# Passes moved from behind a run of four doubles to the head of it, in a DLRM tower on one core

## The chip, the cores and the metric

The kernel runs on one core of a Trainium2 chip. The metric is the device time of one execution in microseconds (us), of which the median of several runs is taken. TensorE (PE) does the matrix products, VectorE (DVE) and ScalarE (ACT) work on its results, GpSimd (POOL) issues the gathers from the embedding tables, and SyncE (SP) issues the other transfers.

## What is computed

A batch of 1024 rows looks up 32 fields of 64 numbers each. For every one of the 496 pairs of fields a 64x64 matrix of the weights stands between the two, which gives one number per pair and row; these and 16 dense numbers go through a tower of three layers.

```python
e = jnp.stack([tbl_0[ids[:, 0]], ..., tbl_31[ids[:, 31]]], axis=1)   # 1024 x 32 x 64
p = e[:, ROW]                                  # the 496 pairs of fields, ROW < COL
q = e[:, COL]
kp = jnp.einsum('bpj,ipj->bpi', p, kernel)     # 64x64 for each pair
z = jnp.sum(kp * q, axis=-1)                   # 1024 x 496
h = jnp.concatenate([z, dense_ctx], axis=1)    # 1024 x 512
h = jnp.maximum(h @ W_top1 + b_top1, 0.0)
h = jnp.maximum(h @ W_top2 + b_top2, 0.0)
y = h @ W_top3
```

## The kernel before

The batch is cut into 4 blocks of 256 rows. Two fields make a tile, so a block has 16 tiles; the 64 tiles of all blocks are gathered by POOL (line 419, four gathers a tile), turned by PE (a transpose, line 644, into `t_ps`) and copied to `rows` by ACT (line 492). In block 0 three tiles are looked up by a product with one-hot rows instead (line 666). From the second block on two tiles are turned at a time.

The pairs are worked off in **pieces**, 62 a block and 248 in all. Each piece is four products on PE into one of the three buffers of `u_ps` (URING), which DVE multiplies with the other field. There are two kinds:

- A **double** (48 a block; line 690, or line 697 for the two of a block that take the fields of a tile with each other, here called self doubles). DVE writes its product to `prod` (lines 607, 610), a ring of 8. Two doubles make a **quad**: PE adds them up along the partitions with a small selector (`add_up`, lines 724 and 730) into `z_ps`.
- A **pass** (14 a block; line 711), where the batch rows stand on the partitions. DVE writes its product to `pass_prod` (line 618), a ring of 3, and ACT adds it up along the row, 16 sums a pass (line 504, `add_along`). When the 14 passes of a block are summed, PE turns the sums (`fold`, line 677), and ACT copies them to `zT` (line 517).

A piece can start on PE when the piece three before it has been multiplied by DVE (`prod_ready`), and when the tiles that it needs stand in `rows`.

The order of all this is fixed when the kernel is built, by the class `Plan`. `step` puts one double after the other; a tile is turned ahead of a piece (`before`) when the next double has no tile, or behind the last double of a run of four (`behind`). BURST is 4: after every fourth double `add_double` puts the passes that are possible (`pass_there`: the tiles are there and fewer than three passes are open), then a tile if one has been gathered, then the two quads of the doubles before (`quads_behind`), and now and then a fold. All engines walk the same list. What PE does between two pairs of quads is called a burst below: four doubles and up to two passes in most cases.

The plan also has a clock of its own. It sets how many sums ACT does at a piece, and after which piece or quad each gather is issued (`in_front`); POOL waits for these marks, and for a free one of the 8 buffers of `nat`.

Of the kernel before, what the change touches and what calls it, by code (L numbers as in the profile page):

```python
# [63 lines left out]
def tile_of(d):  # L64

    return DOUBLES[d][0] if DOUBLES[d][1] is None else DOUBLES[d][1][0]
# [8 lines left out]
BURST = 4  # L75


def quads_behind(n):

    return range(max(0, n // 2 - 3), n // 2 - 1) if n % BURST == BURST - 1 else range(0)  # L80
# [37 lines left out]
def rows_needed(b, tile):  # L118

    return b * TILES + max(FRONT.index(t) if b == 0 and t in FRONT else t for t in range(tile + 1)) + 1  # L120
# [24 lines left out]
class Plan:  # L145
# [96 lines left out]
    def add_double(self):  # L242
        n = self.doubles
        b, d = divmod(n, ND)
        if self.left() and rows_needed(b, tile_of(d)) == len(self.done):
            self.now = max(self.now, self.copied)
        self.append((b, d, None))
        self.doubles += 1
        if n % BURST == BURST - 1:
            if self.pass_there():  # L250
                self.add_pass()
            if self.pass_there() and len(self.open) < 2:
                self.add_pass()
            if len(self.done) < LOOKED_UP and self.next_there() <= self.now - 1.5:
                self.transpose(self.behind[-1])
            self.quads[-1] = quads_behind(n)
            self.now += TURN
            for quad in self.quads[-1]:
                self.now += QUAD
                self.mark(quad + 1)  # L260
            self.now += TURN
            if self.summed and len(self.order) > self.summed[0] + 3:
                self.summed.pop(0)
                self.folded[-1] = self.folds
                self.folds += 1
                self.now += FOLD
# [585 lines left out]
```

## Time and profile before

| | us |
|---|---|
| median of 3 runs | 412.16 |
| lowest and highest | 411.87, 413.91 |
| the profiled execution | 414.25 |
| its span, from the first to the last instruction | 412.5 |

| engine | busy us | share of the span |
|---|---|---|
| PE | 403.7 | 98% |
| DVE | 298.6 | 72% |
| ACT | 259.1 | 63% |
| POOL | 231.6 | 56% |

The profile is one execution, and 1.75 us of its time lie outside the span. It is read from the busiest engine outward: first whether an engine is never idle, then what its steps cost where it is slowed down by another, then whether a moved step finds its inputs there. Times in the trace count from the start of the span. A row of the timeline merges instructions of one kind that follow each other; the start of the next row is a better measure of what they cost than the length of the row, since matmuls overlap.

### The profile page before, as it was taken

How to read it: one execution, taken by the hardware profiler on the slowest of the kernel's cores; microseconds unless marked ns; L12 is line 12 of the kernel's file. 1: busy time of each engine (PE TensorE's matmuls, PEld its weight loads, DVE VectorE, ACT ScalarE, POOL GpSimd, SP SyncE). 2: the span in 40 equal slices, each digit the busy share in tenths (PEclk: the TensorE clock that was granted, in tenths of full speed). 3: DMA queues.
4: the chain of work that ended last, by engine and by line, in shares of the span. 5: the costliest groups of instructions: out<-in, count | busy, mean ns of one | idle time of the engine just before them, and what ended most of it. 6: DMA issues, size and time to landing. Idle time of an engine off the chain costs nothing.

```text
span 412.5 us, 10180 instructions
## 1 busy us (share of the span) xinstructions
PE 403.7 (98%) x3421; PEld 254.4 (62%) x3421; DVE 298.6 (72%) x293; ACT 259.1 (63%) x1874; POOL 231.6 (56%) x251
## 2 busy tenths in 40 slices
PE   7889999999999999999999999999999999999997
PEld 5556656667675766666766665666666566654442
DVE  6776887878788887878979798878879888740000
ACT  6476877667577876764796867719978667002221
POOL 6777777777677757776766777677767200000000
PEclk9998999999999999999999999999999999999999
DMA  6665661131281111211211113111311020000000
GB/s 177 210 200 155 191 221 33 27 77 27 37 219 28 29 19 47 61 28 25 63 42 28 25 25 79 24 27 26 79 25 27 15 51 2 2 2 0 2 0 1
DMA packets 18266, 24.31 MB, mean 59 GB/s; under 512 B 6387, under 2 KB 11767, under 8 KB 17958
## 3 DMA queue, kind: packets, MB, share of 16 engines
q1 hardware_dynamic: 10406, 15.64, 13.0%
q0 software_dynamic: 7808, 8.01, 9.7%
q8 instruction: 28, 0.46, 0.4%
q14 instruction: 24, 0.20, 0.2%
HBM read 19.44 MB, written 0.00 MB: 47 GB/s over the span
## 4 chain that ended last, share of the span: by engine, by line
PE 92%; DMA 3%; POOL 3%; issue 1%; ACT 0%
PE u_ps L690 41%; PE z_ps L724 14%; PE u_ps L711 13%; PE z_ps L730 7%; PE u_ps L771 7%; PE t_ps L644 4%; PE u_ps L791 3%; POOL nat L419 3%; DMA nat<-tbl,ids_sb 2%; PE u_ps L697 2%; DMA ids_sb<-ids 1%; PE t_ps L677 0%; PE u_ps L799 0%; ACT y_sb L571 0%
## 5 line engine op out<-in xcount | busy, mean ns | idle before, releaser
L419 POOL DMA_INDIRECT nat<-tbl,ids_sb x244 | 230.5, 945 | 90.7 <-issue 56.6
L607 DVE TENSOR_TENSOR prod<-u_ps,rows 128x1024 f32<-128x1024 f32 x184 | 213.5, 1218 | 56.7 <-PE u_ps L690 56.7
L504 ACT ACTIVATE pass_prod<-pass_prod 128x64 f32<-128x64 f32 x896 | 214.3, 243 | 22.1 <-DVE pass_prod L618 22.1
L690 PE MATMUL u_ps<-rows,k_sb 64*128 64x256 f32 x1472 | 176.2, 387 | 0.0
L504 ACT ACTIVATION_READ_ACCUMULATOR pass_prod<-pass_prod 128x1 f32 x896 | 169.9, 190 | 0.0
L690 PEld LDWEIGHTS u_ps<-rows,k_sb 64*128 64x128 f32 x1472 | 139.0, 188 | 46.0 <-DVE pass_prod L618 13.4
L618 DVE TENSOR_TENSOR pass_prod<-u_ps,nat 128x1024 f32<-128x1024 f32 x56 | 67.2, 1215 | 1.2 <-PE u_ps L711 1.2
L711 PE MATMUL u_ps<-k_sb,rows 64*128 64x256 f32 x448 | 61.5, 394 | 0.6 <-ACT rows L492 0.6
L724 PE MATMUL z_ps<-prod,sel 128*32 128x512 f32 x512 | 61.6, 598 | 0.0
L492 ACT ACTIVATE rows<-t_ps 128x512 f32<-128x512 f32 (+1 forms) x38 | 19.6, 516 | 54.2 <-PE t_ps L644 54.0
L711 PEld LDWEIGHTS u_ps<-k_sb,rows 64*128 64x128 f32 x448 | 40.6, 186 | 14.6 <-DVE prod L607 9.6
L730 PE MATMUL z_ps<-prod,sel 128*32 128x256 f32 x512 | 30.7, 382 | 0.0
L724 PEld LDWEIGHTS z_ps<-prod,sel 128*32 128x32 f32 x512 | 13.4, 109 | 27.1 <-issue 24.5
L771 PE MATMUL u_ps<-zT,rows 128*128 128x512 f32 x64 | 27.7, 594 | 0.0
L644 PE MATMUL t_ps<-ident,nat 128*128 128x128 f32 x122 | 21.4, 289 | 3.4 <-DMA nat<-tbl,ids_sb 2.8
L730 PEld LDWEIGHTS z_ps<-prod,sel 128*32 128x32 f32 x512 | 15.1, 109 | 12.5 <-issue 2.7
L644 PEld LDWEIGHTS t_ps<-ident,nat 128*128 128x128 f32 x122 | 12.7, 141 | 16.3 <-issue 11.5
L771 PEld LDWEIGHTS u_ps<-zT,rows 128*128 128x128 f32 x64 | 12.1, 190 | 15.2 <-issue 15.2
L562 ACT ACTIVATE k_sb<-u_ps,b_sb 128x512 f32<-128x512 f32 x8 | 5.5, 687 | 22.4 <-PE u_ps L771 22.4
L791 PE MATMUL u_ps<-k_sb,rows 128*128 128x512 f32 x32 | 13.9, 592 | 0.0
L610 DVE TENSOR_TENSOR prod<-u_ps,by_self 128x1024 f32<-128x1024 f32 x8 | 9.8, 1220 | 5.5 <-PE u_ps L697 5.5
L791 PEld LDWEIGHTS u_ps<-k_sb,rows 128*128 128x128 f32 x32 | 6.1, 190 | 7.7 <-issue 7.7
(50 smaller groups left out, 78.9 us busy)
## 6 DMA issues: line engine op xcount, KB each, us to landing
by_self<-rows SPq DMA_DIRECT2D x32, 128.0 KB
nat<-tbl,ids_sb POOLq DMA_INDIRECT x244
k_sb<-kern SPq DMA_DIRECT2D x3, 768.0 KB, 5.6
k_sb<-kern SPq DMA_DIRECT2D x2, 640.0 KB, 5.7
k_sb<-kern SPq DMA_DIRECT2D x1, 1152.0 KB, 5.2
k_sb<-kern SPq DMA_DIRECT2D x2, 512.0 KB
rows<-w SPq DMA_DIRECT2D x1, 1024.0 KB, 6.6
rows<-tbl SPq DMA_DIRECT2D x4, 224.0 KB
```

The source lines that it names most:

```text
L419: pool.indirect_dma_start(nat_of(m, n)[:, h * EMBED:(h + 1) * EMBED], None, tables[f], bass.IndirectOffsetOnAxis(ids_sb[:, col:col + 1], 0 ...
L492: nc.scalar.activation(rows[:, tile:tile + count, cols_of(b)], t_ps[:, 0:count].rearrange("p t n c -> p t (n c)"), ACT.Copy).then_inc(rows ...
L504: op = nc.scalar.activation(of, of, ACT.Copy, accum_out=z_nat[:, b % 2, s, row:row + 1])
L607: nc.vector.tensor_tensor(to, u, by.unsqueeze(1).to_broadcast([P, 2, 2, SIZE]), ALU.mult).then_inc(prod_ready, 1)
L618: nc.vector.tensor_tensor(pass_prod[:, k % CRING], u, by.to_broadcast([P, 2, 2, SIZE]), ALU.mult).then_inc(prod_ready, 1)
L644: op = nc.tensor.transpose(t_ps[:, t, s, :], nat_of(m + t, s), ident[:])
L690: op = nc.tensor.matmul(u[:, h, :], k_sb[part, k_of(d), side, :], rows[part, tile, cols_of(b)], start=True, stop=True)
L711: op = nc.tensor.matmul(u_ps[:, n % URING, h, t, :], rows[part, first + t, at:at + P], k_sb[part, k].rearrange("p s n -> p (s n)"), start= ...
L724: op = nc.tensor.matmul(z_ps[32 * k:32 * k + 32, :, :], sel[:, 30 - 2 * slot:62 - 2 * slot], prod[:, (a + k // 2) % PRING, k % 2], start=s ...
L730: op = nc.tensor.matmul(z_ps[32 * k:32 * k + 32, 0, :], sel[:, 30 - row:62 - row], prod[:, (a + k // 2) % PRING, k % 2, side], start=slot ...
L771: op = nc.tensor.matmul(h_ps(n), w1_sb[:, r * (HID1 // P) + m, :], zT[:, r, cols], start=r == 0, stop=r == ZROWS - 1)
L791: op = nc.tensor.matmul(h_ps(8 + n), w2_sb[:, g * (HID2 // P) + m, :], h1T(g, cols), start=g == 0, stop=g == HID1 // P - 1)
```

## The change

In `add_double` the two conditional calls of `add_pass` move from behind the last double of a run of four to ahead of the first double of the next run. The conditions of the calls are the same, but they are now asked one step later, when tiles may have been turned and sums done in between.

```diff
     def add_double(self):
         n = self.doubles
         b, d = divmod(n, ND)
+        if n % BURST == 0:
+            if self.pass_there():
+                self.add_pass()
+            if self.pass_there() and len(self.open) < 2:
+                self.add_pass()
         if self.left() and rows_needed(b, tile_of(d)) == len(self.done):
             self.now = max(self.now, self.copied)
         self.append((b, d, None))
         self.doubles += 1
         if n % BURST == BURST - 1:
-            if self.pass_there():
-                self.add_pass()
-            if self.pass_there() and len(self.open) < 2:
-                self.add_pass()
             if len(self.done) < LOOKED_UP and self.next_there() <= self.now - 1.5:
                 self.transpose(self.behind[-1])
```

Nothing is added or removed: 248 pieces, 96 quads, 4 folds and the tiles are the same. The lines from 245 on stand one line further down in the changed kernel. In the rows below a double is `x4` of line 690 (691), a pass `x4` of line 711 (712), a self double `x8` of line 697 (698), two quads are `x8` of line 724 (725) or `x16` of line 730 (731), a tile is `x2` of line 644 (645).

PE in block 0, from the last look-up by product on, before:

```order
L666 MATMUL z_ps<-k_sb 64x256 x16
L690 MATMUL u_ps<-rows,k_sb 128x256 x4
L644 MATMUL t_ps<-ident,nat 128x128 x2
L690 MATMUL u_ps<-rows,k_sb 128x256 x4
L711 MATMUL u_ps<-k_sb,rows 128x256 x8
L644 MATMUL t_ps<-ident,nat 128x128 x2
L690 MATMUL u_ps<-rows,k_sb 128x256 x8
L711 MATMUL u_ps<-k_sb,rows 128x256 x4
L644 MATMUL t_ps<-ident,nat 128x128 x2
L690 MATMUL u_ps<-rows,k_sb 128x256 x16
L711 MATMUL u_ps<-k_sb,rows 128x256 x4
L724 MATMUL z_ps<-prod,sel 32x512 x8
```

The same stretch now:

```order
L667 MATMUL z_ps<-k_sb 64x256 x16
L712 MATMUL u_ps<-k_sb,rows 128x256 x4
L691 MATMUL u_ps<-rows,k_sb 128x256 x4
L645 MATMUL t_ps<-ident,nat 128x128 x2
L691 MATMUL u_ps<-rows,k_sb 128x256 x4
L712 MATMUL u_ps<-k_sb,rows 128x256 x4
L645 MATMUL t_ps<-ident,nat 128x128 x2
L691 MATMUL u_ps<-rows,k_sb 128x256 x8
L712 MATMUL u_ps<-k_sb,rows 128x256 x4
L645 MATMUL t_ps<-ident,nat 128x128 x2
L691 MATMUL u_ps<-rows,k_sb 128x256 x16
L725 MATMUL z_ps<-prod,sel 32x512 x8
```

One pass has moved ahead of the first double, and the pass ahead of the first quads has gone behind them; between the last tile of the stretch (`x2`, the third) and the work ahead of it nothing has changed in sum.

PE behind the fold of block 2, before:

```order
L677 MATMUL t_ps<-ident,z_nat 128x128 x2
L690 MATMUL u_ps<-rows,k_sb 128x256 x12
L697 MATMUL u_ps<-rows,k_sb 64x256 x8
L711 MATMUL u_ps<-k_sb,rows 128x256 x4
L730 MATMUL z_ps<-prod,sel 32x256 x16
L690 MATMUL u_ps<-rows,k_sb 128x256 x12
L644 MATMUL t_ps<-ident,nat 128x128 x4
L711 MATMUL u_ps<-k_sb,rows 128x256 x4
L690 MATMUL u_ps<-rows,k_sb 128x256 x4
L711 MATMUL u_ps<-k_sb,rows 128x256 x4
L730 MATMUL z_ps<-prod,sel 32x256 x16
```

The same stretch now:

```order
L678 MATMUL t_ps<-ident,z_nat 128x128 x2
L712 MATMUL u_ps<-k_sb,rows 128x256 x4
L691 MATMUL u_ps<-rows,k_sb 128x256 x12
L698 MATMUL u_ps<-rows,k_sb 64x256 x8
L731 MATMUL z_ps<-prod,sel 32x256 x16
L712 MATMUL u_ps<-k_sb,rows 128x256 x4
L691 MATMUL u_ps<-rows,k_sb 128x256 x12
L645 MATMUL t_ps<-ident,nat 128x128 x4
L712 MATMUL u_ps<-k_sb,rows 128x256 x4
L691 MATMUL u_ps<-rows,k_sb 128x256 x4
L731 MATMUL z_ps<-prod,sel 32x256 x16
```

The pass of each burst stands at its head, and the burst with two tiles in its middle has four pieces ahead of them in place of three.

ACT in the same place, from the copy of that fold on (line 517 or 518; `x40` are 40 sums of passes, and behind them stands the copy of the two tiles), before:

```order
L517 ACTIVATE zT<-t_ps 128x256
L504 ACTIVATE pass_prod,z_nat<-pass_prod 128x64 x40
L492 ACTIVATE rows<-t_ps 128x2x256
L504 ACTIVATE pass_prod,z_nat<-pass_prod 128x64 x14
L513 ACTIVATE zT<-z_ps 128x256
```

The same stretch now:

```order
L518 ACTIVATE zT<-t_ps 128x256
L505 ACTIVATE pass_prod,z_nat<-pass_prod 128x64 x44
L493 ACTIVATE rows<-t_ps 128x2x256
L505 ACTIVATE pass_prod,z_nat<-pass_prod 128x64 x4
L514 ACTIVATE zT<-z_ps 128x256
```

Four more sums stand ahead of the copy of the two tiles.

## Rows read from the trace of the kernel before

**Rows 1.** The chain that ended last, share of the span by engine (page)

```profile
PE 92%; DMA 3%; POOL 3%; issue 1%; ACT 0%
```

**Rows 2.** Waits: who waited for whom, us in total, times, longest us

```profile
DVE prod L607 <- PE u_ps L690: 56.7, 47, 3.5
...
PE t_ps L644 <- DMA nat<-tbl,ids_sb: 2.8, 2, 2.1
```

**Rows 3.** Timeline of PE, bursts of five, six, four: start, us, instructions

```profile
90.61 3.72 PE L690 MATMUL u_ps<-rows,k_sb 64*128 64x256 f32 x32
94.21 1.14 PE L711 MATMUL u_ps<-k_sb,rows 64*128 64x256 f32 x8
...
97.72 3.72 PE L690 MATMUL u_ps<-rows,k_sb 64*128 64x256 f32 x32
...
105.38 2.86 PE L690 MATMUL u_ps<-rows,k_sb 64*128 64x256 f32 x24
...
342.73 3.72 PE L690 MATMUL u_ps<-rows,k_sb 64*128 64x256 f32 x32
...
348.23 3.73 PE L690 MATMUL u_ps<-rows,k_sb 64*128 64x256 f32 x32
```

**Rows 4.** Timeline of DVE over the first of these bursts

```profile
91.80 4.62 DVE L607 TENSOR_TENSOR prod<-u_ps,rows 128x1024 f32<-128x1024 f32 x4 [1.40 <-PE u_ps L690]
```

**Rows 5.** Timeline of PE behind the fold of block 2

```profile
277.62 2.86 PE L690 MATMUL u_ps<-rows,k_sb 64*128 64x256 f32 x24
...
284.36 2.86 PE L690 MATMUL u_ps<-rows,k_sb 64*128 64x256 f32 x24
287.15 0.66 PE L644 MATMUL t_ps<-ident,nat 128*128 128x128 f32 x4
287.74 1.13 PE L711 MATMUL u_ps<-k_sb,rows 64*128 64x256 f32 x8
288.70 1.07 PE L690 MATMUL u_ps<-rows,k_sb 64*128 64x256 f32 x8
...
290.57 1.72 PE L730 MATMUL z_ps<-prod,sel 128*32 128x256 f32 x28
```

**Rows 6.** Timeline of PE, a burst that begins with a self double

```profile
213.86 1.09 PE L697 MATMUL u_ps<-rows,k_sb 64*64 64x256 f32 x16
214.88 2.86 PE L690 MATMUL u_ps<-rows,k_sb 64*128 64x256 f32 x24
...
220.39 2.86 PE L690 MATMUL u_ps<-rows,k_sb 64*128 64x256 f32 x24
```

**Rows 7.** Timeline of ACT, the two copies around the sums behind that fold

```profile
277.72 0.39 ACT L517 ACTIVATE zT<-t_ps 128x256 f32<-128x256 f32 x1 [1.58 <-PE t_ps L677]
...
287.90 0.60 ACT L492 ACTIVATE rows<-t_ps 128x512 f32<-128x512 f32 x1 [0.26 <-PE t_ps L644]
```

**Rows 8.** Timeline of PE in block 0 (PEld is its weight load)

```profile
23.20 0.44 PE L644 MATMUL t_ps<-ident,nat 128*128 128x128 f32 x2 [0.76 <-DMA nat<-tbl,ids_sb]
...
26.43 0.20 PEld L644 LDWEIGHTS t_ps<-ident,nat 128*128 128x128 f32 x2 [0.40 <-DMA nat<-tbl,ids_sb]
...
31.71 0.44 PE L644 MATMUL t_ps<-ident,nat 128*128 128x128 f32 x2 [2.06 <-DMA nat<-tbl,ids_sb]
...
37.33 1.03 PE L711 MATMUL u_ps<-k_sb,rows 64*128 64x256 f32 x8
...
40.14 0.44 PE L644 MATMUL t_ps<-ident,nat 128*128 128x128 f32 x2
...
47.61 2.00 PE L690 MATMUL u_ps<-rows,k_sb 64*128 64x256 f32 x16
...
61.49 2.86 PE L690 MATMUL u_ps<-rows,k_sb 64*128 64x256 f32 x24
...
69.67 3.72 PE L690 MATMUL u_ps<-rows,k_sb 64*128 64x256 f32 x32
```

**Rows 9.** Stretches of the trace: busy us of each engine, PEclk (granted clock), DMA share

```profile
33.00:36.40 3.40, 3.40 (x19) 2.79 (x18) 2.45 (x2) 3.40 (x30) 2.49 (x4) 0.50 0.54 126
```

## The prediction

> **What bounds the kernel now.** I read the chain of work that ended last first: PE has 92% of it [rows 1]. Then the waits. DVE waits for PE 47 times, about once a burst, while PE's own matmuls are held up by an outside party only twice in earnest, both times by a gather in block 0 [rows 2]. So PE sets the time, and the question is what a burst costs on PE and whether the new order changes that. ACT and POOL matter only where PE finds something missing.
>
> **What a burst costs.** I take every burst from the start of its first piece to the start of the first piece behind its two quads. Four doubles: 348.23 - 342.73 = 5.50 us. Six pieces: 105.38 - 97.72 = 7.66 us. Five pieces with a pair of tiles in front of the quads: 97.72 - 90.61 = 7.11 us [rows 3]; the pair alone costs 287.74 - 287.15 = 0.59 us [rows 5], which leaves 6.52 us. The fifth piece costs 1.02 us and the sixth 1.14 us, where the first four come at (94.21 - 90.61) / 4 = 0.90 us apiece. The reason is DVE. It needs (4.62 - 1.22) / 3 = 1.13 us a piece (1.22 us is the mean of one of its products), and starts 1.19 us behind PE, at 91.80 [rows 4]. The fifth piece may start when the second is multiplied, at 91.80 + 1.13 + 1.22 = 94.15; it starts at 94.21 [rows 3]. This rule does not ask which piece is the pass: a pass and a double cost DVE the same, and PE too (four matmuls of the same size). So `P d d d d` costs what `d d d d P` costs, 6.52 us, and `P P d d d d` what `d d d d P P` costs, 7.66 us. In between DVE falls idle for over 1 us in each burst (1.40 us in [rows 4]), so no burst hands a debt to the next.
>
> **The change part by part.** Since nothing is added, the sum is a tally of bursts by kind, 47 before and 47 after, by the order of the changed program. I leave tiles and folds out of the prices, as they are the same in number.
>
> 1. *Ordinary bursts.* Four pieces: 7 before, 6 after (-5.50). Five: 16 and 18 (+13.04). Six: 7 and 6 (-7.66). Both lists hold 150 pieces. Sum -0.12 us.
>
> 2. *Bursts with a self double* (without the last of all and the one in block 0). Before they hold 30 pieces: one `ddds`, two `dddsP`, two `sdddP`, one `sdddPP`. After they hold 32: one `PPddds`, two `Pddds`, two `Psddd`, one `PPsddd`. Growing from four pieces to six costs 7.66 - 5.50 = 2.16, less about 0.1 since `ddds` is itself dearer: +2.04. For the order inside a burst I use that a self double costs 214.88 - 213.86 = 1.02 us at the head, and that `sdddP` costs 220.39 - 213.86 = 6.53 us with its quads [rows 6] and `dddsP` 284.36 - 277.62 = 6.74 us [rows 5]: a self double inside a burst costs 0.2 us more than one at its edge, as PE changes its tile size twice more. `Pddds` moves it to the edge (twice -0.2), `Psddd` moves it inside (twice +0.2), and in the six-piece burst DVE is the limit anyway. These four cancel. Sum +2.04 us.
>
> 3. *Bursts with two tiles in the middle* (five). Before `ddd`, tiles, `P d P`: 290.57 - 284.36 = 6.21 us up to the quads, and the piece ahead of the last costs about 0.88 us from 288.70 on [rows 5]. After, `Pddd`, tiles, `P d`: with two pieces behind the tiles in place of three, DVE is no longer caught up with, and I get four pieces at 3.65 (5.50 less the quads' 1.85), 0.59, and two at 0.97 and 0.96: 6.17. Sum 5 x -0.04 = -0.2 us.
>
> 4. *Block 0 from the third late tile on.* The five bursts from 31.71 to 69.67 take 37.96 us and hold 26 pieces of this stretch; after they hold 24. The pass at 37.33 goes from ahead of the quads to behind the tile at 40.14: the first burst loses 0.86 us. The second, 47.61 - 40.14 = 7.47 us now, gets a pass ahead of its self double and a lone double between a tile and the quads, two edges more: +0.2. The third and fourth keep their price. The fifth, 69.67 - 61.49 = 8.18 us, loses a piece, of six: -0.87 [rows 8]. Sum -1.5 us.
>
> 5. *Block 0 ahead of that.* A pass moves ahead of the first double and fills the 0.76 us in which PE waits for the tile at 23.20. But the work up to the next tiles is the same, and these come with their gathers: at about 26.4, where the weight load waits 0.40 us for one, and at 31.71 after 2.06 us [rows 8]. PE arrives 0.8 us earlier at the first of them and waits there instead. Gain 0.
>
> 6. *Cover.* The quads now follow the fourth double directly. They read products of the doubles of the burst before, and by the ring of three all of those are done when the last double starts: 0. DVE's waits for the ring of `prod` get earlier quads, not later ones: 0. The copies of the tiles by ACT: behind the fold of block 2 ACT has 40 sums between the copy at 277.72 and that at 287.90, busy all the way but for 0.26 us, and the double that needs the tiles starts at 288.70, 0.2 us behind the end of the copy at 288.50 [rows 5, 7]. Now there are 44 sums, (287.90 - 0.26 - 278.11) / 40 = 0.24 us each, +0.96 us; PE gets there one piece (0.86 us) later. The copy then ends at about 289.2 and the double is due at 289.4. Cost 0, with 0.6 us as the bound if the copy is late by its own length. The tile now asked for at about 39.3 in place of 40.14 [rows 8] may find its gather not landed: 0 to 0.85 us.
>
> **Sum.** -0.12 + 2.04 - 0.2 - 1.5 = about +0.2 us. Against the profiled execution, 414.25 us (span 412.5 and 1.75 around it), that is 414.4. Against the median, 412.16, it is 412.3 us. The bounds are -0.5 (every edge in steps 2 to 4 comes out cheaper) and +1.7 (both waits of step 6 in full).
>
> **Why profile and median differ** matters for the range. In the profiled execution the granted clock is 0.50, the 1.2 GHz level, from 33.0 to 36.4 [rows 9], just behind the wait of 2.06 us at 31.71 [rows 8]. The stretch holds 3.4 us, so half the clock costs about 1.7 us of work. The slowest timed run, 413.91, lies as far above the two others as that. So I read two of three runs as without the drop. The Trainium skill ("TensorE: Matmul & The Clock Gate", section "HAM oscillation — how this bites in real kernels") says that gaps in which PE waits for a transfer bring the clock down behind them; the trace agrees with its one drop behind its longest gap.
>
> **The rivals.**
>
> *The clock drop becomes the rule (slower).* Step 5 puts a wait of 0.8 us at about 25.6, closer ahead of the one of 2.06 us than the wait at 23.2 was. If PE's pause counts as longer for it, most executions drop and the median is that of the profile: 414.25 + 0.1, 414.3 us. Against it: between the two waits PE still works for over 3 us without a pause, and the long wait itself is unchanged. It decides only if the drop turns up in two of three runs. I give it 0.13.
>
> *The new places turn PE's inputs late (slower by little).* Both waits of step 6 come due, and 412.16 + 0.2 + 1.45 = 413.8 us. For it speaks the margin of 0.2 us at 288.70, against it that ACT is not ahead of a needed tile by so little anywhere else I found. 0.07.
>
> *The stall of the fifth and sixth piece goes away (faster).* If a burst that starts with a pass let PE run to the end without waiting for DVE, each five-piece burst would save 1.02 - 0.90 = 0.12 us and each six-piece burst 0.36: 22 x 0.12 + 8 x 0.36 = 5.5 us, 406.7. It needs DVE to start or step faster with a pass, and nothing in the rows says so. 0.04.
>
> *Tile sizes.* The Trainium skill ("TensorEngine Tiling (Array Packing)", section "Key Properties") says that changing the tiling mode drains PE. The rows show that price as about 0.1 us an edge (step 2). A rival by it: if each edge beside a lone piece or a self double cost twice as much, steps 2 and 4 would add some 1 us: 413.3. 0.04.
>
> *The change does nothing at all:* the orders differ in nearly every burst, so this is only possible in effect, and then it is the forecast.
>
> **How the numbers follow.** The forecast, a tie at 412.3 us, has 0.72. The range leaves out the 5.5 us gain and takes in the clock on both sides: from 411.2 (the lowest run, 411.87, less the bound of 0.5) to 414.5 (the profile's 414.25 with the sum). A change under 0.5%, 2.06 us, is about what a measurement of this kernel can't tell from none. Slower by more needs the clock: 0.12 of its 0.13. Faster by more: 0.05. Within: 0.83.
>
> **What would show it.** In the trace after, `P d d d d` with its quads should take 6.5 us, `P P d d d d` 7.7 us, `Psddd` 6.7 us, and DVE should wait once a burst as now. The tile at 31.71 should stay at its place. The last quads should end within 0.7 us of where they end now, the clock drop left aside. I would be wrong if PE showed waits at quads, if a double waited for a copy by ACT, or if DVE began a burst later behind a pass than 1.2 us after PE.

## Result and profile after

The changed kernel takes 418.93 us in the median of five executions (417.89 to 428.49), the kernel before, measured beside it, 412.65 (411.87 to 413.91, five). The highest, 428.49 us, came in a slower state of the chip and doesn't enter the ratio. That ratio is 1.0131, with a 95% interval from 1.0095 to 1.0167: the change costs 5.4 us (3.9 to 6.9), where a tie was forecast. The profiled execution took 420.19 us, with a span of 418.4, which is 5.9 us more than that of before.

The page of after gives the chain of work that ended last, share of the span by engine:

```profile
PE 92%; ACT 5%; DMA 1%; DVE 1%; issue 1%; POOL 0%; POOLq 0%; ACTq 0%
```

ACT had 0% of it in [rows 1], and has 5% now. The largest of PE's waits in after, and the wait of DVE that answers to [rows 2] (us in total, times, longest us):

```profile
PE u_ps L712 <- ACT rows L493: 5.7, 6, 1.7
...
DVE pass_prod L619 <- PE u_ps L712: 60.2, 44, 3.5
```

The first row is new in its size. Before, the same wait (passes, line 711, for ACT's copies, line 492) came once, in block 0:

```profile
PE u_ps L711 <- ACT rows L492: 0.6, 1, 0.6
```

That one is still there as the sixth. Five others are added. A line of waits that was a footnote now holds nearly all of the loss. DVE waits once a burst as before, only now for the pass at its head.

The bursts themselves are as forecast. Timeline of PE in after, a burst of five pieces with tiles ahead of it, and one with a self double behind its pass:

```profile
90.50 1.14 PE L712 MATMUL u_ps<-k_sb,rows 64*128 64x256 f32 x8
91.47 3.76 PE L691 MATMUL u_ps<-rows,k_sb 64*128 64x256 f32 x32
95.16 1.94 PE L731 MATMUL z_ps<-prod,sel 128*32 128x256 f32 x32
97.03 1.13 PE L712 MATMUL u_ps<-k_sb,rows 64*128 64x256 f32 x8
...
215.41 1.14 PE L712 MATMUL u_ps<-k_sb,rows 64*128 64x256 f32 x8
216.47 1.09 PE L698 MATMUL u_ps<-rows,k_sb 64*64 64x256 f32 x16
...
222.14 1.13 PE L712 MATMUL u_ps<-k_sb,rows 64*128 64x256 f32 x8
```

97.03 - 90.50 = 6.53 us for `P d d d d` and its quads (6.52 forecast), and 222.14 - 215.41 = 6.73 us for `Psddd` (6.7 forecast); they answer to [rows 3] and [rows 6].

**Where the waits are.** With two tiles turned in the middle of a burst, the step from the first product of the turning to the next piece took 0.59 us everywhere before [rows 5]. Timeline of PE in after at the tile pair T38 (T38 is the pair of tiles 38 and 39, counted over all blocks; block 2), then of ACT there:

```profile
203.02 0.66 PE L645 MATMUL t_ps<-ident,nat 128*128 128x128 f32 x4
204.52 1.14 PE L712 MATMUL u_ps<-k_sb,rows 64*128 64x256 f32 x8 [0.84 <-ACT rows L493]
```

```profile
203.78 0.60 ACT L493 ACTIVATE rows<-t_ps 128x512 f32<-128x512 f32 x1 [0.90 <-PE t_ps L645]
```

The step is now 1.50 us, 0.91 more. ACT had nothing else to do (it was idle for 0.90 us until the tiles were turned), started 0.76 us behind the turning's start, took 0.60, and the pass started 0.15 us behind its end. This is the bare length of turning and copying, which nothing covers. Before, the pass in this place could start at once, as it needed older tiles; only the double behind it needed the new ones.

In block 3 ACT comes on top. Timeline of PE at T54 (the place of [rows 5]), at T56 and at T58, then of ACT at T54 and T56:

```profile
290.30 0.66 PE L645 MATMUL t_ps<-ident,nat 128*128 128x128 f32 x4
292.68 1.13 PE L712 MATMUL u_ps<-k_sb,rows 64*128 64x256 f32 x8 [1.73 <-ACT rows L493]
...
301.13 0.66 PE L645 MATMUL t_ps<-ident,nat 128*128 128x128 f32 x4
301.71 1.92 PE L725 MATMUL z_ps<-prod,sel 128*32 128x512 f32 x16
304.77 2.00 PE L712 MATMUL u_ps<-k_sb,rows 64*128 64x256 f32 x16 [1.13 <-ACT rows L493]
...
311.13 1.92 PE L725 MATMUL z_ps<-prod,sel 128*32 128x512 f32 x16
313.67 1.13 PE L712 MATMUL u_ps<-k_sb,rows 64*128 64x256 f32 x8 [0.61 <-ACT rows L493]
```

```profile
291.72 0.24 ACT L505 ACTIVATE pass_prod<-pass_prod 128x64 f32<-128x64 f32 x1
291.96 0.57 ACT L493 ACTIVATE rows<-t_ps 128x512 f32<-128x512 f32 x1
...
304.05 0.57 ACT L493 ACTIVATE rows<-t_ps 128x512 f32<-128x512 f32 x1
```

At T54 the copy starts 1.66 us behind the turning in place of 0.76, with a sum directly ahead of it, and the step is 2.38 us: 1.79 lost. At T56 and T58 two quads (1.86 us) stand between the turning and the pass, enough to cover a copy that is on time, but the copy starts 2.92 us behind the turning at T56. The step of the quads is 304.77 - 301.71 = 3.06 for the pair of quads, 1.2 us longer than 1.86, and 313.67 - 311.13 = 2.54 at T58, 0.68 longer. The five sum to 0.90 + 0.91 + 1.79 + 1.19 + 0.68 = 5.47 us. The last quad of the last block starts 5.92 us later than before (371.99 and 366.07). Of that, 0.48 us are there before the first full burst: the tile that waits longest for its gather starts at 32.19 in place of 31.71. From this tile on, the two executions differ by 339.80 - 334.36 = 5.44 us, and the five waits are all of it.

**Which passes.** Where the condition for a pass is asked at the head of a run, a tile pair may have been turned a moment ago, behind the last double. `pass_there` counts tiles as there once they are turned, and asks nothing about the copy; only doubles wait for it in the plan's clock. So 16 passes of the changed order stand directly behind the turning of a pair that they need themselves, with at most two quads and a fold between, and none did before. Two are in block 1, seven each in blocks 2 and 3. At the three mid-burst pairs of those blocks (T38, T42, T54) nothing stands between, and these always wait. T56 and T58 wait where ACT is behind. The others have their copy in time.

### The profile page after: what moved, and what is told of

Same layout as the page of the kernel before. It is cut to its first block, busy times and chain, and to the rows that moved or that the text cites. A ratio compares the mean times of both kernels' runs of the same rounds, so it can differ in the third digit from the quotient of the medians.

```text
span 418.4 us, 10180 instructions
## 1 busy us (share of the span) xinstructions
PE 405.1 (97%) x3421; PEld 254.7 (61%) x3421; DVE 298.7 (71%) x293; ACT 259.7 (62%) x1874; POOL 231.5 (55%) x251
## 4 chain that ended last, share of the span: by engine, by line
PE 92%; ACT 5%; DMA 1%; DVE 1%; issue 1%; POOL 0%; POOLq 0%; ACTq 0%
PE u_ps L691 38%; PE z_ps L725 13%; PE u_ps L712 13%; PE z_ps L731 7%; PE u_ps L772 7%; PE t_ps L645 4%; ACT pass_prod L505 4%; PE u_ps L792 3%; PE u_ps L698 2%; PE z_ps L667 2%; PE t_ps L667 2%; DMA nat<-tbl,ids_sb 1%; ACT rows L493 1%; DVE pass_prod L619 1%; PE u_ps L634 0%
## 5 line engine op out<-in xcount | busy, mean ns | idle before, releaser
L691 PEld LDWEIGHTS u_ps<-rows,k_sb 64*128 64x128 f32 x1472 | 139.7, 188 | 31.0 <-DVE prod L608 11.6
L514 ACT ACTIVATE zT<-z_ps 128x256 f32<-128x256 f32 x4 | 1.5, 383 | 19.3 <-PE z_ps L731 19.3
```

The source lines that it names most:

```text
L691: op = nc.tensor.matmul(u[:, h, :], k_sb[part, k_of(d), side, :], rows[part, tile, cols_of(b)], start=True, stop=True)
```

## Experiments

On most chips that these experiments ran on, all kernels, the kernel before too, had medians of 490 to 502 us (last section), so each ratio below is against the kernel before on the same chip, and times of different chips are not compared. On two, those of `p_blocks23` and `s1_head_settled`, the kernel before takes 412.9 and 412.7 us; these carry the sizes. On the other chips it is the traces that decide, since a piece that waits for a copy has a mark that was the same on both kinds of chip: it starts 0.14 to 0.15 us behind the copy's end.

The theory: **PE waits for the copy of tiles that a pass, now at the head, needs at once; in block 3 the copy is late in addition, because ACT has sums queued ahead of it.** Rivals: the bursts themselves or block 0 got dearer; the copies are late for a reason other than the sums; the waits are hidden by slack elsewhere.

**1. The change in blocks 2 and 3 only** (`p_blocks23`).

```diff
-        if n % BURST == 0:
+        if n % BURST == 0 and n >= 2 * ND:
             if self.pass_there():
                 self.add_pass()
...
         if n % BURST == BURST - 1:
+            if n < 2 * ND - 1:
+                if self.pass_there():
+                    self.add_pass()
...
```

> The change in blocks 2 and 3 alone (from the 96th double on; in blocks 0 and 1 the passes stay at the end of each run). In block 2 no pass then stands right behind the turning of its own tiles without the quads between, in block 3 the list is that of the changed kernel. Theory A: the waits of PE for a copy at pieces 193, 200 and 206 remain (1.79 + 1.19 + 0.68 = 3.7 us in the trace of after), those at 131 and 147 do not occur: 0.9% over before. Theory B, by which each burst that begins with a pass costs something: about half of the loss, 0.65%, spread over all bursts of these blocks.

Measured: 417.30 us against 412.88, ratio 1.0107 [1.0070, 1.0144]. PE's waits for the copies, then its timeline at T38 and T54:

```profile
PE u_ps L717 <- ACT rows L498: 4.0, 4, 1.7
```

```profile
200.62 0.66 PE L650 MATMUL t_ps<-ident,nat 128*128 128x128 f32 x4
201.20 1.13 PE L717 MATMUL u_ps<-k_sb,rows 64*128 64x256 f32 x8
...
287.28 0.66 PE L650 MATMUL t_ps<-ident,nat 128*128 128x128 f32 x4
289.67 1.13 PE L717 MATMUL u_ps<-k_sb,rows 64*128 64x256 f32 x8 [1.73 <-ACT rows L498]
```

The three waits of block 3 are those of after to 0.02 us (1.80, 1.21, 0.67, together 3.68). Of the loss, 4.4 us (2.9 to 5.9 by the interval) against 3.7 of waits, the greater part sits in block 3. T38 and T42 don't wait here (step 0.58), although they are in block 2 and the new placement holds: the passes of this block have not run ahead by one, since the blocks before were placed as before. So it isn't the head of the run as such that costs, but whether the pass there needs the pair just turned.

The other half, the change in blocks 0 and 1 only (`r4_blocks01`, with the two conditions turned round), fell on a chip of the 495 us kind:

> The change in blocks 0 and 1 alone: passes at the head of each run there, at the end in blocks 2 and 3. In these blocks of after PE waits for no copy except in block 0 as before. Theory A: the time of before, within 0.3%. Theory B, by which each burst that begins with a pass costs something: about half of the loss, 0.65% over before.

Measured: 496.86 against 495.77 us, ratio 1.0038 [0.9993, 1.0083]. The interval holds both no loss and 0.8%. In its trace the step behind T38 is 0.59 us, and behind T42 the pass starts at 282.86, ahead of the copy at 283.29, so it doesn't wait for it. So the two waits of block 2 come neither with the one half nor with the other; by the orders of the four programs, they need passes that have run ahead since the first blocks and a head placement in block 2.

**2. The head of the run, but only with passes whose tiles are older** (`s1_head_settled`; the same kernel as `e1_head_settled`, `r1_head_settled` and `q1_head_settled`).

```diff
-        return b < BLOCKS and len(self.open) < CRING and rows_needed(b, pass_of(j)[0] + 1) <= len(self.done)
+        return b < BLOCKS and len(self.open) < CRING and rows_needed(b, pass_of(j)[0] + 1) <= (len(self.done) if b == 0 else self.settled)
...
         self.order.append(what)
+        self.settled = len(self.done)
```

> The changed kernel (passes still at the head of each run), but from block 1 on a pass may only use tiles that were turned before the piece ahead of it; no pass is placed right behind the turning of its own tiles. Theory A (the loss is five waits of PE for ACT's copy of a tile just turned, 5.47 us in the trace of after): all five are gone, 412.7 to 413.2 us, PE waits on ACT's copies under 1 us in all. Theory B (a burst that begins with a pass is dearer by itself, or the loss lies in the start of block 0): the heads stay and so does the loss, about 418 us.

> The changed kernel (passes still at the head of each run), but from block 1 on a pass may only use tiles that were turned before the piece ahead of it; no pass stands right behind the turning of its own tiles. Theory A (the loss is five waits of PE for ACT's copy of a tile just turned, 5.47 us in the trace of after): all five are gone, the time is within 0.3% of before, PE waits on ACT's copies under 1 us in all. Theory B (a burst that begins with a pass is dearer by itself, or the loss lies in the start of block 0): the heads stay and so does the loss, about 1.3% over before.

> The changed kernel with passes still at the head of each run, but from block 1 on a pass may only use tiles that were turned before the piece ahead of it; no pass stands right behind the turning of its own tiles. Theory A (the loss is PE's waits for ACT's copy of tiles just turned): all five waits are gone and the time is that of before within 0.3%, 412.5 to 414 us. Theory B (a burst that begins with a pass is dearer by itself): the heads stay and so does the loss, 1.3% over before.

> The changed kernel with passes still at the head of each run, but from block 1 on a pass may only use tiles that were turned before the piece ahead of it. Theory A (the loss is PE's waits for ACT's copy of tiles just turned): all five waits are gone and the time is that of before within 0.3%. Theory B (a burst that begins with a pass is dearer by itself): the heads stay and so does the loss, 1.3% over before.

Measured in `s1_head_settled`: 414.59 us against 412.70, ratio 1.0048 [1.0033, 1.0063]. The loss falls from 5.4 to 2.0 us (1.4 to 2.6 by the interval). PE's waits for copies ahead of doubles (line 693) in its trace, then its timeline at the two places in block 3 where they are, T54 and T58:

```profile
PE u_ps L693 <- ACT rows L495: 1.1, 2, 0.7
```

```profile
285.65 0.66 PE L647 MATMUL t_ps<-ident,nat 128*128 128x128 f32 x4
286.24 1.13 PE L714 MATMUL u_ps<-k_sb,rows 64*128 64x256 f32 x8
287.79 1.13 PE L693 MATMUL u_ps<-rows,k_sb 64*128 64x256 f32 x8 [0.42 <-ACT rows L495]
...
309.70 1.13 PE L714 MATMUL u_ps<-k_sb,rows 64*128 64x256 f32 x8
311.50 1.13 PE L693 MATMUL u_ps<-rows,k_sb 64*128 64x256 f32 x8 [0.67 <-ACT rows L495]
```

The pass waits nowhere any more (285.65 to 286.24 is 0.59 us), and all five waits of after are gone. In their place two *doubles* behind a covering pass wait for ACT in block 3: 287.79 - 286.24 = 1.55 us and 1.80 us in place of 0.97, together 1.4 us. One piece covers a copy that is on time, not one that is late. That leaves 0.6 us of the 2.0 without a place, no more than the interval allows for.

The other three runs of this kernel, on chips of the 490 us kind, gave 0.9996 [0.9937, 1.0055], 1.0087 [1.0034, 1.0139] and 1.0087 [1.0054, 1.0120]. The trace of the last (`q1_head_settled`) has the step of 0.59 us to the pass at every mid-burst pair, so no pass waits, but doubles behind the passes do. PE's waits for copies ahead of doubles in it:

```profile
PE u_ps L693 <- ACT rows L495: 7.6, 4, 3.3
```

The same waits in the kernel before with the addition of experiment 6 (`w_fill`), on such a chip:

```profile
PE u_ps L692 <- ACT rows L494: 4.1, 4, 2.3
```

At T22 in `q1_head_settled` the double starts 151.79 - 148.70 = 3.09 us behind the pass in place of 0.97, and 0.14 us behind the copy's end. The other two traces of this kernel have 5.7 and 7.1 us of such waits, the other trace of the order of before (`e8_fill`) 4.3. So on these chips too one piece doesn't cover a late copy. In single traces that is 1.4 to 3.5 us more than with the order of before, where 0.9% is 4.3 us; the rest has no place.

**3. The kernel before without its cover** (`u_no_cover`; the same kernel as `e6_no_cover` and `r3_no_cover`). It takes only the covering pass away and leaves the passes at the end of the run.

```diff
-                if self.left() and self.pass_there():
+                if self.left() and self.pass_there() and len(self.done) <= TILES:
```

> The kernel before, but from block 1 on no pass is put between the turning of a pair of tiles in the middle of a burst and the first double that needs them (five places). Passes stay at the end of the runs. Theory A: each place then shows a wait of about 0.9 us of PE for the copy, 5 x 0.9 = 4.5 us, about 417 us, without any pass at a head. Theory B: no pass stands at a head, so the time is that of before, 412.7 us.

> The kernel before, but from block 1 on no pass is put between the turning of a pair of tiles in the middle of a burst and the first double that needs them (five places). Passes stay at the end of the runs. Theory A: each place shows a wait of about 0.9 us of PE for the copy, 5 x 0.9 = 4.5 us, 1.1% over before, without any pass at a head. Theory B: no pass stands at a head, so the time is that of before.

> The kernel before, with one rule changed: from block 1 on, the pass that stands between a tile pair turned in the middle of a run of doubles and the double that needs it (at T22, T26, T38, T42 and T54) is left to the end of the run. If the lost cover is what costs time, TensorE waits for ScalarE's copy at each of the five: the step behind the turning takes 1.5 us in place of 0.59, 0.9 us each, together 4.5 us, so about 417.2 us, a ratio to the kernel before of 1.009 to 1.012. If the waits are hidden by slack that TensorE has later anyway, the steps grow but the time stays within 0.3% of before. If TensorE doesn't wait there, steps of 0.59 us and the time of before.

Measured in `u_no_cover`: 502.14 against 496.94 us, ratio 1.0098 [1.0061, 1.0135]; the earlier two 1.0040 [0.9994, 1.0087] and 1.0113 [1.0019, 1.0206]. Timeline of PE at T54, where now a double follows:

```profile
361.29 0.66 PE L644 MATMUL t_ps<-ident,nat 128*128 128x128 f32 x4
362.79 1.14 PE L690 MATMUL u_ps<-rows,k_sb 64*128 64x256 f32 x8 [0.84 <-ACT rows L492]
```

The step is 1.50 us, as at T38 in after, with ACT not behind. The three traces have the longer step at all five pairs (1.49 to 3.84 us); where it is over 1.5, the copy itself started 1.19 to 3.10 us behind the turning in place of 0.75, and the double 0.14 to 0.15 us behind its end. So with the passes where they were, a missing cover makes PE wait at each of the five, and the time is longer by 1.0 and 1.1% in two runs; in the third, 0.4%, the interval just holds no loss. In two of three, at least, the waits were not hidden by slack.

**4. ACT copies first** (`w_copy_first`; the same kernel as `e2_copy_first`, `r2_copy_first`, `t_copy_first`, `v_copy_first` and `x_copy_first`). PE and DVE as in after; ACT's program in blocks 2 and 3 has the copy one piece ahead of the sums.

```diff
+            early = 2 * (ND + NP)
...
-                for m, count in PLAN.before[n]:
+                for m, count in PLAN.before[n] if n < early else []:
...
-                for which in PLAN.sums[n]:
-                    add_along(*which)
+                if n < early:
+                    for which in PLAN.sums[n]:
+                        add_along(*which)
...
+                if n >= early:
+                    if n + 1 < PIECES:
+                        for m, count in PLAN.before[n + 1]:
+                            rows_out(m, count)
+                    for which in PLAN.sums[n]:
+                        add_along(*which)
```

> The changed kernel, and in blocks 2 and 3 ACT copies a turned pair of tiles ahead of the sums that stand at the same or the preceding piece, in place of behind them. Theory A with its second half (in block 3 the copy comes late because sums are queued ahead of it on ACT): the waits at pieces 200 and 206 (1.19 and 0.68 us) vanish and that at 193 falls from 1.79 to 0.9 us, a gain of 2.8 us over the changed kernel, about 415.7 us. If the copies were late because PE turns the tiles late, nothing changes: 418.5 us.

> The changed kernel, and in blocks 2 and 3 ACT copies a turned pair of tiles ahead of the sums that stand at the same or the preceding piece, in place of behind them. Theory A with its second half (in block 3 the copy comes late because sums are queued ahead of it on ACT): the waits at pieces 200 and 206 (1.19 and 0.68 us) vanish and that at 193 falls from 1.79 to 0.9 us: 2.8 us of the loss come back and 2.7 us stay, about 0.7% over before. If the copies were late because PE turns the tiles late, nothing comes back: 1.3% over before.

> The kernel after, with one thing changed: in the blocks 2 and 3 ScalarE's program has the copy of a tile pair ahead of the sums of the piece that stands there and of the piece before, in place of behind them; TensorE's and VectorE's programs are those of after. If the copies are late because of the sums queued ahead of them, the waits of after in block 3 shrink: behind T54 from 1.79 to about 0.9 us (what is left is the turning and the copy itself, as at T38 and T42 in block 2), behind T56 from 1.19 and behind T58 from 0.68 to about 0; together 2.7 us, so some 416.2 us, a ratio to the kernel before of 1.007 to 1.010. If the copies are late for another reason (the bank in which tiles are turned, or ScalarE waiting for something else), the three waits stay and the ratio stays at 1.013. If the sums, now later, hold up VectorE's product buffers, new waits of VectorE and so of TensorE come in their place and the ratio stays at 1.013 or rises, with waits of VectorE for ScalarE in block 3.

> The same kernel as in the run before of this name: in the blocks 2 and 3 ScalarE's program has the copy of a tile pair ahead of the sums of the piece that stands there and of the piece before. Copies late because of the sums queued ahead: behind T54 the wait falls from 1.79 to about 0.9 us, behind T56 from 1.19 and behind T58 from 0.68 to about 0; together 2.7 us less than after, a ratio to the kernel before of 1.007 to 1.010. Late for another reason: the three waits stay, ratio 1.013. Sums that now come late hold up VectorE's buffers: waits of VectorE for ScalarE in block 3 and a ratio of 1.013 or above.

> The kernel after with ScalarE's copies of tile pairs ahead of the sums in blocks 2 and 3, once more. Copies late because of the sums queued ahead: TensorE's steps behind T54 1.5 us (2.38 in after), behind Q73 and Q75 0.97 (2.17 and 1.65), a ratio to the kernel before of 1.007 to 1.010. Late for another reason: those steps as in after, ratio 1.013.

> The kernel after with ScalarE's copies of tile pairs ahead of the sums in blocks 2 and 3, once more. Copies late because of the sums queued ahead: the steps of TensorE behind T54 1.5 us (2.38 in after), behind Q73 and Q75 0.97 (2.17 and 1.65), 2.7 us less than after, a ratio to the kernel before of 1.007 to 1.010. Late for another reason: those steps as in after, ratio 1.013. Sums that now come late hold up VectorE's buffers: waits of VectorE for ScalarE in block 3 and a ratio of 1.013 or above.

Six runs, all on chips of the 490 us kind: ratios 1.0038 [0.9999, 1.0076], 1.0068 [1.0022, 1.0115], 1.0068 [1.0028, 1.0108], 1.0041 [0.9987, 1.0095], 1.0072 [1.0046, 1.0098] and 1.0002 [0.9964, 1.0040]. All lie below after's 1.0131, but three of the intervals reach into that of after, and after itself was not run on such a chip. Timeline of PE at T54 and T56 in `w_copy_first`, and of ACT at T54:

```profile
365.24 0.65 PE L653 MATMUL t_ps<-ident,nat 128*128 128x128 f32 x4
366.73 1.13 PE L720 MATMUL u_ps<-k_sb,rows 64*128 64x256 f32 x8 [0.84 <-ACT rows L493]
...
376.29 0.66 PE L653 MATMUL t_ps<-ident,nat 128*128 128x128 f32 x4
376.87 1.92 PE L733 MATMUL z_ps<-prod,sel 128*32 128x512 f32 x16
380.45 1.78 PE L720 MATMUL u_ps<-k_sb,rows 64*128 64x256 f32 x14 [1.65 <-DVE prod L616]
```

```profile
365.99 0.60 ACT L493 ACTIVATE rows<-t_ps 128x512 f32<-128x512 f32 x1 [0.40 <-issue]
```

Half of it came as the theory wants. At T54 the step is 1.49 us in three of the six traces (1.89 and twice 3.00 in the others) in place of 2.38, and behind T58 the quads' step falls to its usual size in all six. Behind T56 the wait stays or grows in five of six. The row there names DVE, but the copy ended at 380.30, 0.15 us ahead of the pass: the mark of the copy. The reason is in ACT's timeline in another of the six (`x_copy_first`), the copy of T56, which was turned at 368.54:

```profile
371.55 0.19 ACT L505 ACTIVATION_READ_ACCUMULATOR pass_prod<-pass_prod 128x1 f32 x1
371.64 0.57 ACT L493 ACTIVATE rows<-t_ps 128x512 f32<-128x512 f32 x1
```

A sum stands directly ahead of it still: those of earlier pieces are not done. ACT's program is a fixed list, and moving the copy forward by one piece's sums is not enough where ACT is behind by more. The third reading on record, that sums which now come late hold up DVE's buffers, shows in one trace of the six: in `x_copy_first` DVE waits 3.7 us for them, once.

**5. Half of the sums of block 3 left out** (`y_half_sums`). This takes the backlog away and leaves every order as in after; the rows of z concerned are not computed.

```diff
                 for x in range(first, end):
+                    if b == BLOCKS - 1 and x % 2 == 0:
+                        continue
```

> The kernel after with half of the row sums of the passes of block 3 left out of ScalarE's program (those rows of z then hold what block 1 left), everything else in its order. If ScalarE's backlog of sums makes the copies late, TensorE's steps behind T54 (2.38 us in after), Q73 (2.17) and Q75 (1.65) fall to 1.5 or less, 0.97 and 0.97, and after's 5.5 us of waits to 2.7, a ratio to the kernel before of 1.006 to 1.010. The waits of 0.9 behind T38 and T42, in block 2, stay as they are. If the copies are late for another reason, all five steps are those of after and the ratio stays at 1.013.

Measured: 499.40 against 496.44 us, ratio 1.0061 [1.0019, 1.0102]. Timeline of PE at T54 and T56, of ACT at T56:

```profile
365.26 0.65 PE L647 MATMUL t_ps<-ident,nat 128*128 128x128 f32 x4
366.75 1.13 PE L714 MATMUL u_ps<-k_sb,rows 64*128 64x256 f32 x8 [0.84 <-ACT rows L493]
...
376.20 0.65 PE L647 MATMUL t_ps<-ident,nat 128*128 128x128 f32 x4
376.78 1.92 PE L727 MATMUL z_ps<-prod,sel 128*32 128x512 f32 x16
378.76 2.27 PE L714 MATMUL u_ps<-k_sb,rows 64*128 64x256 f32 x16
```

```profile
377.79 0.60 ACT L493 ACTIVATE rows<-t_ps 128x512 f32<-128x512 f32 x1 [2.01 <-PE t_ps L647]
```

With ACT idle ahead of each copy, T54's step is 1.49 us, that of T38, and the pass behind T56 starts 1.98 us behind the quads' start in place of 3.06 (1.86 without a wait). Behind T58 the quads' step is 1.86. T38 and T42 in block 2, whose sums are all there, stay at 1.49. The trace to set this against is that of experiment 4, since after has none on such a chip: there, with all sums in ACT's program, the pass behind T56 started 3.58 us behind the quads' start and waited for its copy. What block 3 loses beyond the bare 0.9 us at T54 is ACT's backlog of sums. The share of it in the time, 0.9 + 1.19 + 0.68 = 2.8 us, could not be weighed on a chip where the kernel before takes 412 us.

**6. A fill for the clock** (`w_fill`, and the same kernel as `e8_fill`): the kernel before with eight more products of the identity on PE ahead of the tile at 31.71 [rows 8].

```diff
+        if m == 7:
+            self.fill[m] = 8
```

> The kernel before, and 8 matmuls of the identity with itself ahead of the tile at 31.7 us, in the 2.06 us in which PE waits for its gather (their result is overwritten). It tests the reading that the half clock behind that wait costs 1.7 us in some executions. If so: clock 1.00 throughout in the profile and 1.0 to 1.7 us less than before in its slower executions, about 411.8 us in the median. If not: 412.7 us.

> The kernel before with eight more products of the identity on TensorE ahead of T7, where it waits for a gather. If the clock falls to 0.50 because TensorE stands still there, it stays at 1.0 in every execution, the time is that of the faster executions of before (411.9 to 412.5) and the ratio 0.996 to 0.999. If the drop isn't set by that wait, it comes as before and the ratio is 1.000 or, with the fill on the path, 1.001.

Measured in `w_fill`: 497.57 against 495.94 us, ratio 1.0023 [0.9987, 1.0059], and 1.0029 [1.0000, 1.0058] in the earlier run. It settles nothing: on these chips the mean granted clock is 0.955 to 0.976 in every execution of either kernel, and in `w_fill` it is 0.50 already from 28 to 32 us, ahead of the place in question. No kernel tried here is faster than the kernel before beyond its interval.

## Why the prediction was wrong

**Steps 1 to 5, the bursts and block 0, held.** `P d d d d` 6.53 us, `Psddd` 6.73, `P P d d d d` 7.64 (7.7 forecast). In step 3 the five bursts with two tiles in the middle take 8.07 us before and, where they don't wait, 8.07 after: no gain where 0.04 us each was forecast. In block 0 the tile at 31.71 is at 32.19, behind the same gather. All told, from this tile on the last quad is 5.44 us later, and 5.47 of it are waits, which leaves nothing for the structure, against the +0.2 of the sum. Two numbers of the working are not what their own terms give, and change nothing: the double at T54 would be due at 288.70 + 0.86 = 289.56, not 289.4, and the lower end of the range is 411.87 - 0.5 = 411.4, not 411.2.

**Step 6, "Cover", failed, and it alone.** It priced the copies at T54 by the *double* behind the pass ("the double is due at 289.4. Cost 0") and took for granted that the pass in between still covers. Yet the pass itself now needs the pair. One question was left out: of each pass that moved, which tiles it needs, and how long ago they were turned. The order of the changed program answers it without a chip, and it would have shown 16 such passes. The size of ACT's delay was right, by contrast: four more sums, +0.96 us forecast; the copy at T54 starts 1.66 us behind the turning in place of 0.75 (287.90 - 287.15 in [rows 5, 7]), +0.91. And that ACT is ahead of a needed tile "by so little" at one place only was true of before, not of the new order. Of the forecast's own signs, the last quads within 0.7 us of their place failed; a *double* waiting for a copy did not come in after, since it was passes that waited.

**The right rival was there, at 0.07 and too small.** "The new places turn PE's inputs late" is the mechanism that came, but it was priced at 413.8 us, with one place in block 3 and one in block 0, while five places wait in the blocks 2 and 3, each of them longer (0.68 to 1.79 us) than the bound of 0.6 us. That bound was "the copy's own length", 0.6; the least that an uncovered turning costs is 0.9 us (0.76 to the copy's start, 0.60 for the copy, 0.14 to the pass, less the 0.59 of the turning), and ACT's queue adds to it without a bound in that row. The range ended at 414.5 us, which was the case of the clock; no case in it had more than two waits.

**The clock rival did not come.** The mean granted clock is 0.995 in the profiled execution of after and 1.000 in the four others. In the profiled one the clock is halved behind the tile at 32.19, where it was before [rows 9]; the stretch of 3.5 us (columns: stretch, its length, busy us of PE, PEld, DVE, ACT and POOL, PEclk, DMA share, GB/s):

```profile
32.19 0.69 PE L645 MATMUL t_ps<-ident,nat 128*128 128x128 f32 x2 [2.19 <-DMA nat<-tbl,ids_sb]
```

```profile
32.10:35.60 3.50, 3.41 (x16) 2.56 (x18) 0.66 (x1) 2.68 (x22) 2.83 (x3) 0.51 0.35 83
```

The forecast's reading of profile against median stands in part. Of the seven executions of the kernel before beside `p_blocks23`, the one at a mean clock of 0.996 took 414.48 us and the six at 1.000 took 411.85 to 413.08. But the ten beside `s1_head_settled`, all at 1.000, reach up to 413.56, so the time of 413.91 alone doesn't show a drop. The loss has nothing to do with it: at 1.000, executions of after took 417.89 us and more.

**What stays open:** nothing that stands clear of the noise is left of the loss beyond the waits (5.4 us, from 3.9, against 5.5 of waits; 4.4, from 2.9, against 3.7; 2.0, from 1.4, against 1.4). Open are the part of the 0.9% that experiment 2 loses on two chips of the 490 us kind beyond its doubles' waits, and the weight of ACT's backlog in the time of a chip where the kernel before takes 412 us, which was never measured by itself.

## What to carry to other kernels

When work is moved past the step that makes its input, ask of each moved piece which input it needs and how long ago that was made, and price the whole chain from producer through copy to consumer (0.9 us here), not the copy alone. A piece that fills a gap does so only as long as it doesn't need what the gap waits for: placing such pieces earlier lets them run ahead until they do. An engine that is off the critical path and has its own fixed list (here ACT and its sums) adds its backlog to every such chain.

## What the runs showed of the hardware

**One program, two kinds of chip.** On the chips of the 490 to 502 us kind DVE's product takes 1.22 us and the weight load 0.19 us, as elsewhere. The loss is for the most part between the instructions, and the mean granted clock is lower too (0.94 to 0.98 in nearly all executions). The weight loads of the doubles, kernel before in its profiled execution at 412.5 us, then the kernel of experiment 6 at 497.5 us (busy us, mean ns, idle before and what ended it):

```profile
L690 PEld LDWEIGHTS u_ps<-rows,k_sb 64*128 64x128 f32 x1472 | 139.0, 188 | 46.0 <-DVE pass_prod L618 13.4 <-issue 9.4 <-DVE prod L607 8.5
```

```profile
L692 PEld LDWEIGHTS u_ps<-rows,k_sb 64*128 64x128 f32 x1472 | 139.9, 189 | 92.2 <-issue 41.7 <-DVE prod L609 25.2 <-DVE pass_prod L620 10.9
```

Idle time that ended with nothing but "issue", that is, with nothing that the profile shows, is 41.7 us in place of 9.4. This is the highest of the 16 traces of this kind; in the others it is 11.6 to 39.5 us. Nor is it PE alone: the chain that ended last has a part on this kind of chip that neither before nor after has, 6 to 11% for another core or an unknown queue, here in `w_fill`:

```profile
PE 75%; ACT 8%; another core or an unknown queue 8%; DVE 4%; issue 4%; POOL 0%; ACTq 0%; POOLq 0%; DVEq 0%
```

DVE, ACT and POOL wait there as well for something that the profile can't name. The cause wasn't tried. One chip number gave both kinds, five minutes apart (`q1_head_settled` and `s1_head_settled`).

**A wait alone does not halve the clock.** PE waited 2.06 and 2.19 us for the same gather in the profiled executions of before and after, and the granted clock fell to half (1.2 GHz) behind it. In `p_blocks23` it waited longer, and the clock stayed at full speed (2.4 GHz); timeline of PE and the stretch behind it:

```profile
32.61 0.44 PE L650 MATMUL t_ps<-ident,nat 128*128 128x128 f32 x2 [2.90 <-DMA nat<-tbl,ids_sb]
```

```profile
32.00:36.00 4.00, 3.39 (x30) 2.93 (x32) 1.84 (x2) 2.91 (x24) 2.97 (x4) 1.00 0.28 71
```

The rule of the forecast, gaps bring the clock down behind them (the Trainium skill, "TensorE: Matmul & The Clock Gate", section "HAM oscillation — how this bites in real kernels"), holds for two of these three traces and not for the longest gap. What decides between them no run here shows.
